# Attention beside expert tiles on one core: contiguous products for TensorE's sums, two more pairs in the first stretch, four tiles a step

## What is computed

```python
q = (x @ Wq + bq).reshape(B, T, H, Dh)                    # H = 16, Dh = 8
kv = ((x @ Wdown + bdown) @ Wup + bup).reshape(B, T, H, 2 * Dh)
k, v = jnp.split(kv, 2, axis=-1)
q, k = apply_rope(q), apply_rope(k)
att = jnp.einsum('bthd,btgd->bthg', q, k) / jnp.sqrt(Dh)
att = jax.nn.softmax(att, axis=-1)                        # over g, the heads
out = jnp.einsum('bthg,btgd->bthd', att, v)
return out.reshape(B, T, D) @ Wout + bout
```

```python
for e in range(E):
    h = gelu(x @ W_in[e] + b_in[e])
    out = out + combine[..., e, None] * (h @ W_out[e] + b_out[e])
```

## Time and profile before

| | us |
|---|---|
| median of three runs (1363.98 to 1368.10) | 1367.02 |
| the profiled execution | 1364.03 |
| its span in the trace | 1362.1 |
| TensorE busy, whole span | 1123.0 (82%) |
| VectorE busy | 831.2 (61%) |
| GpSimd busy | 796.9 (59%) |
| ScalarE busy | 596.3 (44%) |
| granted TensorE clock, mean | 0.954 of full |

### The profile page before, as it was taken

The page is one execution under the profiler, slowest core; times in us unless marked ns, Lnnn a source line. Parts: engine busy times, 40 slices in busy tenths (PEclk is TensorE's granted clock), DMA queues, the critical chain, the costliest instruction groups (busy, mean ns, idle before and its releaser), DMA issues.

```text
span 1362.1 us, 19492 instructions
## 1 busy us (share of the span) xinstructions
PE 1123.0 (82%) x6608; PEld 873.0 (64%) x6608; DVE 831.2 (61%) x1139; ACT 596.3 (44%) x1529; POOL 796.9 (59%) x613
## 2 busy tenths in 40 slices
PE   1448999999998988988783458899869999999975
PEld 1432222223887776777672457799868899899965
DVE  7946999997999999999998975111121000000038
ACT  0120011112766566656564448800005666656667
POOL 4605877873889899989881004767533445445520
PEclk9998999999999999999995779999989999999988
DMA  5471332131454554554445420199995767777747
GB/s 174 161 298 64 112 115 111 51 102 33 143 165 145 155 147 147 162 150 152 136 130 196 155 92 30 53 296 327 317 338 145 204 203 202 205 204 202 203 187 216
DMA packets 119955, 225.63 MB, mean 166 GB/s; under 512 B 16709, under 2 KB 80101, under 8 KB 117810
## 3 DMA queue, kind: packets, MB, share of 16 engines
q1 hardware_dynamic: 102164, 188.16, 44.9%
q0 software_dynamic: 17344, 35.57, 7.2%
q10 hardware_dynamic: 350, 0.67, 0.2%
HBM read 157.19 MB, written 67.14 MB: 165 GB/s over the span
## 4 chain that ended last, share of the span: by engine, by line
PE 42%; POOL 24%; DVE 11%; DMA 10%; ACT 6%; issue 6%; SPq 1%; POOLq 0%; ACTq 0%; DVEq 0%
PE ps L721 14%; POOL BG L259 12%; POOL y_tok L429 12%; PE ps L679 9%; PE ps L692 9%; DMA TPB<-in_kpad 5%; DVE XN L893 3%; DMA FF<-sorted_x 2%; PE ps L803 2%; DVE stats L863 2%; PE ps L805 2%; PE ps L668 1%; PE ps L730 1%; DMA xt_d<-xT 1%; DVE X L1037 1%
## 5 line engine op out<-in xcount | busy, mean ns | idle before, releaser
L429 POOL DMA_INDIRECT y_tok<-FF,yidx x284 | 306.9, 1081 | 206.0 <-ACT FF L497 146.0
L421 POOL DMA_INDIRECT sorted_x<-XN,idx x256 | 278.8, 1089 | 90.1 <-issue 89.0
L692 PE MATMUL ps<-FF 128*128 128x128 f32 x2272 | 278.8, 276 | 0.0
L692 PEld LDWEIGHTS ps<-FF 128*128 128x128 f32 x2272 | 266.9, 193 | 14.4 <-issue 4.3
L679 PE MATMUL ps<-FF 128*128 128x256 f32 x1136 | 273.8, 385 | 0.0
L488 ACT ACTIVATE FF<-ps,FF 128x256 f32<-128x256 f32 x568 | 230.2, 481 | 34.0 <-PE ps L679 33.1
L679 PEld LDWEIGHTS ps<-FF 128*128 128x128 f32 x1136 | 208.5, 194 | 23.3
L721 PE MATMUL ps<-BG,cst 128*128 128x512 f32 x208 | 193.3, 1097 | 0.0
L1146 DVE TENSOR_TENSOR BG<-BG,ps 128x512 f32<-128x512 f32 x16 | 10.6, 686 | 290.6 <-PE ps L837 290.4
L259 POOL TENSOR_TENSOR BG<-TPB 128x2048 f32<-128x2048 f32 x38 | 171.6, 4515 | 25.6 <-DVE BG L1028 13.6
L1016 DVE TENSOR_TENSOR BG<-BG,TPB 128x1024 f32<-128x1024 f32 x128 | 147.8, 1215 | 0.0
(11 more groups left out here) (185 smaller groups left out, 1676.7 us busy)
## 6 DMA issues: line engine op xcount, KB each, us to landing
FF<-in_moe SPq DMA_DIRECT2D x142, 514.0 KB
TPB<-in_kpad SPq DMA_DIRECT2D x22, 1024.0 KB, 7.8
sorted_x<-TPB SPq DMA_DIRECT2D x36, 516.0 KB, 4.1
FF<-sorted_x SPq DMA_DIRECT2D x142, 129.0 KB
FF<-in_kpad SPq DMA_DIRECT2D x10, 1024.0 KB
BG<-y_tok SPq DMA_DIRECT2D x8, 1024.0 KB, 6.6
X<-y_tok SPq DMA_DIRECT2D x8, 1024.0 KB, 6.5
y_tok<-FF,yidx POOLq DMA_INDIRECT x284, 3.2
```

The lines of the kernel that those rows point to most:

```text
L421: pool.indirect_dma_start(sorted_x[layer], bass.IndirectOffsetOnAxis(ap=idx[:, k, j:j + 1], axis=0), XN[:, j, :], None).then_inc(s_sc, 16)
L429: pool.indirect_dma_start(y_d[layer], bass.IndirectOffsetOnAxis(ap=yidx[:, G % 4, r:r + 1], axis=0), ys[:, G % 4, r * D:(r + 1) * D], None ...
L692: t = pe.matmul(psY[:, r * P:(r + 1) * P], hT[:, G % 2, m, r * P:(r + 1) * P], wc[:, G % 4, HID + m * D:HID + (m + 1) * D], start=False, s ...
```

## The change

TensorE's part grows. Products are laid out so that every pass of the score sum reads contiguous runs: ScalarE's evacuation of a projection tile now reorders `q` and `k` to feature-major (and `v` of the first 13 pairs to head-major) by two copies in place of one, and `own_product` writes its products feature by feature. The weighted products of pairs 0 to 12 (`PVS = 13`) are written in eight blocks of 512 and summed by TensorE too (`sum_values`, in the bank `psO`); VectorE reduces the remaining 512 to 256 in the next step (`finish_heads`). The scores have one bank, `psS`, in place of two, so a score sum waits until the one before has been read. `OWN` goes from 13 to 15 and `T_FIRST` from 12 to 14. From `T_FIRST` on a step has four tiles. Of the pairs from 15 on, GpSimd makes both half products of the even ones, and only the first of the odd ones; VectorE makes the second itself, in two instructions. GpSimd's first half product now waits for the weighted products of pair `b - 2`, not for its scaled heads.

```diff
-OWN = 13
-T_FIRST = 12
+OWN = 15
+PVS = OWN - 2
+T_FIRST = 14
+PER_STEP = 4
 def tiles_of(b):
-    f0, f1 = (7 * (b - T_FIRST + i) // 2 for i in range(2))
-    return [f for f in range(max(f0, 0), min(f1, NF))]
+    f0 = PER_STEP * (b - T_FIRST)
+    return [f for f in range(max(f0, 0), min(f0 + PER_STEP, NF))]
+def on_pool(b):
+    return 0 if b < OWN else 2 - b % 2
...
-        psS = [psH[2], psH[3]]
+        psO, psS = psH[2:4]
...
                 if b + 1 < NPAIR:
                     pool.wait_ge(s_qkv, 2 * (b + 1) + 2)
-                    pool.wait_ge(s_on, b - 1)
+                    pool.wait_ge(s_pv, b - 1)
                     qk_product(pool, b + 1, 0).then_inc(s_pp, 1)
                 for f in late[:2]:
                     scatter_outputs(0, f)
-                if b + 1 < NPAIR:
+                if b + 1 < NPAIR and on_pool(b + 1) == 2:
...
-                act.copy(qkv[:, m % 4, t, :], bank[:, 0:3 * D]).then_inc(s_qkv, 1)
+                if m < OWN:
+                    act.copy(qkv[:, m % 4, t, 0:2 * D].rearrange("p (a e h) -> p a e h", a=2, e=DH),
+                             bank[:, 0:2 * D].rearrange("p (a h e) -> p a e h", a=2, e=DH))
+                    v, vp = qkv[:, m % 4, t, 2 * D:3 * D], bank[:, 2 * D:3 * D]
+                    if m < PVS:
+                        v, vp = v.rearrange("p (g e) -> p g e", g=H), vp.rearrange("p (e g) -> p g e", e=DH)
+                    act.copy(v, vp).then_inc(s_qkv, 1)
+                else:
+                    act.copy(qkv[:, m % 4, t, :], bank[:, 0:3 * D]).then_inc(s_qkv, 1)
...
                 if G == 1:
                     pe.wait_ge(s_sub, OWN)
+                    pe.wait_ge(s_on, PVS)
...
             def sum_products(b):
                 pe.wait_ge(s_own, b + 1)
-                wait(pe, s_sub, b - 1)
-                pr = prod[:, b % 2, :].rearrange("p (n e) -> p e n", e=DH)
+                wait(pe, s_sub, b)
+                pr = prod[:, b % 2, :].rearrange("p (t e n) -> p e t n", t=2, e=DH)
...
+            def sum_values(b):
+                pe.wait_ge(s_pv, b + 1)
+                wait(pe, s_on, b)
+                pv = prodv.rearrange("p (i n) -> p i n", i=DH)
+                for i in range(DH):
+                    t = pe.matmul(psO[:, :], ident, pv[:, i, :], start=(i == 0), stop=(i == DH - 1))
+                t.then_inc(s_O, 1)
...
+                    if c == 0 and 2 <= b < PVS + 2:
+                        sum_values(b - 2)
                     if c == 0 and 3 <= b < NPAIR + 3:
                         heads_T(b - 3)
...
-                    dve.wait_ge(s_pp, 2 * (b - OWN) + 2)
+                    if on_pool(b) == 1:
+                        dve.wait_ge(s_qkv, 2 * b + 2)
+                        qk_product(dve, b, 1, 0, H // 2)
+                        link(qk_product(dve, b, 1, H // 2, H // 2))
+                    dve.wait_ge(s_pp, sum(on_pool(i) for i in range(b + 1)))
...
+            def finish_heads(b):
+                dve.wait_ge(s_O, b + 1)
+                link(dve.tensor_reduce(O, psO[:, :].rearrange("p (i n) -> p n i", i=2), AX.X, ALU.add))
+                scale_heads(b, O)
...
+                if 2 <= b < PVS + 2:
+                    finish_heads(b - 2)
                 if b >= 1:
-                    weighted(b - 1)
+                    (weighted_for_pe if b - 1 < PVS else weighted)(b - 1)
```

More of the change, by code:

```diff
@@ L212, in mixed_layers @@
         s_S = sem("scores_psum")
+        s_O = sem("heads_psum")
         s_sub = sem("scores_ready")
@@ L717, in sum_products @@
                 pe.wait_ge(s_own, b + 1)
-                wait(pe, s_sub, b - 1)
-                pr = prod[:, b % 2, :].rearrange("p (n e) -> p e n", e=DH)
+                wait(pe, s_sub, b)
+                pr = prod[:, b % 2, :].rearrange("p (t e n) -> p e t n", t=2, e=DH)
                 for e in range(DH):
-                    t = pe.matmul(psS[b % 2][:, :], ident, pr[:, e, :], start=(e == 0), stop=(e == DH - 1))
+                    t = pe.matmul(psS[:, :].rearrange("p (t n) -> p t n", t=2), ident, pr[:, e, :, :],
+                                  start=(e == 0), stop=(e == DH - 1))
                 t.then_inc(s_S, 1)
+            def sum_values(b):
[5 more added lines that the diff above has]
+                t.then_inc(s_O, 1)
             def qkv_tile(m, t, bank=psQ):
@@ L984, in own_product @@
                 dve.wait_ge(s_qkv, 2 * b + 2)
+                n = DH // 2
                 for t in range(2):
-                    for h0 in (0, H // 2):
-                        i = qk_product(dve, b, t, h0, H // 2)
+                    for e0 in (0, n):
+                        q = qkv[:, b % 4, t, e0 * H:(e0 + n) * H].rearrange("p (e h) -> p e h", e=n)
+                        k = qkv[:, b % 4, t, D + e0 * H:D + (e0 + n) * H].rearrange("p (e g) -> p e g", e=n)
+                        o = t * 2048 + e0 * H * H
+                        i = dve.tensor_tensor(
+                            prod[:, b % 2, o:o + n * H * H].rearrange("p (e h g) -> p e h g", e=n, h=H),
+                            q[:, :, :, None].to_broadcast([P, n, H, H]), k[:, :, None, :].to_broadcast([P, n, H, H]),
+                            ALU.mult)
                 i.then_inc(s_own, 1)
@@ L1007, in add_heads, with pair_sums, scale_heads, weighted_for_pe @@
                 dve.tensor_tensor(xv, xv, psA[:, 0:256], ALU.add).then_inc(s_xup, 1)
+            def pair_sums(b):
+                dve.wait_ge(s_exp, b + 1)
+                return mark(dve.tensor_reduce(Sm, S[:, b % 2, :].rearrange("p (n g) -> p n g", g=H), AX.X, ALU.add))
+            def scale_heads(b, heads):
+                wait(dve, s_ot, b - 2)
+                dve.tensor_tensor(On[:, b % 3, :].rearrange("p (n e) -> p n e", e=DH), heads.rearrange("p (n e) -> p n e", e=DH),
+                                  Rc[:, :, None].to_broadcast([P, 2 * H, DH]), ALU.mult).then_inc(s_on, 1)
+            def weighted_for_pe(b):
+                summed = pair_sums(b)
+                wait(dve, s_O, b)
+                for t in range(2):
+                    v = qkv[:, b % 4, t, 2 * D:3 * D].rearrange("p (g e) -> p g e", g=H)
+                    sc = S[:, b % 2, t * 256:(t + 1) * 256].rearrange("p (h g) -> p g h", h=H)
+                    pv = prodv.rearrange("p (g t h e) -> p t g h e", g=H, t=2, h=H)
+                    for g0 in (0, H // 2):
+                        n, g1 = H // 2, g0 + H // 2
+                        i = dve.tensor_tensor(pv[:, t, g0:g1, :, :],
+                                              sc[:, g0:g1, :, None].to_broadcast([P, n, H, DH]),
+                                              v[:, g0:g1, None, :].to_broadcast([P, n, H, DH]), ALU.mult)
+                i.then_inc(s_pv, 1)
+                dve.wait_ge(s_v, summed)
+                link(dve.reciprocal(Rc, Sm))
+            def finish_heads(b):
+                dve.wait_ge(s_O, b + 1)
+                link(dve.tensor_reduce(O, psO[:, :].rearrange("p (i n) -> p n i", i=2), AX.X, ALU.add))
+                scale_heads(b, O)
             def weighted(b):
-                dve.wait_ge(s_exp, b + 1)
-                summed = mark(dve.tensor_reduce(Sm, S[:, b % 2, :].rearrange("p (n g) -> p n g", g=H), AX.X, ALU.add))
+                summed = pair_sums(b)
                 for t in range(2):
```

8 lines of the change are left out of this document (3 added, 5 removed).

## The result

| | before | after |
|---|---|---|
| median, us | 1365.59 (8 runs, 1362.06 to 1369.27) | 1371.60 (8 runs, 1370.17 to 1375.26) |
| span of the profiled execution, us | 1362.1 | 1369.0 |
| first `hidden` at, us | 335.5 | 351.65 |
| last scatter of the layer at, us | 719.99 | 718.68 |
| combination begins at, us | 727.34 | 734.83 |

The ratio is 1.0048, 95% interval 1.0031 to 1.0065, so the changed kernel is slower by a little. The prediction had said 1352 us, faster than before; the measured time still lies inside its range of 1336 to 1373, but on the slower side of the kernel before. Behind the combination nothing changed: 1362.1 - 727.3 = 634.8 us before, 1369.0 - 734.8 = 634.2 now. So all of it happened ahead of that point.

A forecast was written before the change was run, and what follows sets the result against it. GpSimd was taken to bound the part with expert tiles: 35.0 us won there less 20.8 lost at its start gains 14.2, from 1364.03 to 1349.8 profiled; with the median 3.0 above, 1352 us was predicted, range 1336 to 1373.

The forecast's parts named there:

- What bounds the kernel: TensorE, 97% busy, from 106 to 338 us (stretch 1); GpSimd from 355 to 700 us (stretch 2), 19.43 us a step.
- The contiguous passes: Score sum on TensorE: reading contiguous runs, a pass takes 0.43 us instead of 0.918, a group of 16 takes 6.9.
- rival (d): Matmul passes stay at 0.918 us, a step before the expert tiles is 33 us, time about 1570; chance 0.02.
- VectorE in stretch 1: Attention steps before the tiles: VectorE's work falls to 13.1 us a step; its saving of 3.7 isn't on the path.
- ScalarE's copies: Evacuation of a projection tile: two copies take 1.0 us instead of one of 0.48, adding 0.5 a step for TensorE.
- The start of the tiles: The first `hidden` comes at 356.3 us instead of 335.5, behind the last value sum: 20.8 us later.
- The two steps laid out by hand: Steps with expert tiles: VectorE loses 3.65 us at its subtraction, GpSimd's later product costs nothing; 38.5 us for two.
- The rule of the Trainium skill: VectorE instructions with two SBUF inputs and GpSimd instructions reading SBUF take turns, whole instructions each; descriptor writing is inferred unaffected.
- Rival (a): VectorE's own halves collide with GpSimd's product in every second step: 21.3 us a step, 1383 us; chance 0.18.
- The forecast's step: A step with four expert tiles takes 19.5 us, bounds 18.7 and 20.1.
- What ends the layer: Last scatter at 705.8 us, then the load of its rows, then the combination; VectorE's own way ends earlier, at 711.
- The sign by which to tell: VectorE's two half products at 1.2 us each speak for the forecast, one of 4 to 5 for Rival (a).

## Why the prediction was wrong, point by point

- **What bounds the kernel** was right: GpSimd in stretch 2, TensorE in stretch 1. The run with all products on GpSimd at four tiles a step took 41.4 for two steps with 0.1 us idle.
- **The contiguous passes**, 0.43 each, 6.9 a group: 6.87 measured, for both sums. The rival (d) fell at once.
- **VectorE in stretch 1** was right in size (it waits 4.2 us a step). The prediction saw that the saving isn't on the path and that the price is, but didn't work out what the value sum costs: 14 to 16 us at the first `hidden`.
- **ScalarE's copies** were a mis-sized term: 1.0 taken, 0.64 measured (0.37 + 0.27), and 0.53 from start to end, hardly more than the 0.48 of the one copy. The nearer rows would have been that copy, from the same bank, and the kernel's other copies of 256 columns out of PSUM, of 0.37 to 0.40 us (L480, L497 and L508 before), not the later ones of 0.61 and 0.43. The step came out at 17.09 instead of 17.45, pair 14's sum ended at 343.55 instead of 348.3, and the first `hidden` stood at 351.65 instead of 356.3. This error was in the kernel's favour.
- **The start of the tiles**: 16.1 us later instead of 20.8.
- **The two steps laid out by hand** carry the failed step. Counted from the release of GpSimd's second product (462.36 - 42.86 = 419.50, one period before the row shown), VectorE's halves began at 25.06 (forecast 25.2) and GpSimd was ready at 25.84 (forecast 26.1 to 26.6, a little late). The times are right, and so is that GpSimd is ready while VectorE is in its halves. Wrong is the overlap that was concluded from them, "the product then runs under the reduction and costs nothing". It treats two instructions as one hold. The prediction had itself said that the share is held for a whole instruction, and the rows bear it out: the first half ended, the waiting GpSimd product got its turn, and the second half waited 4.3 us. For the two steps: 38.5 + 4.3 = 42.8, and 42.86 measured; with the collision taken away 38.65 and 38.47.
- **The rule of the Trainium skill** (SBUF — State Buffer, Who interferes with whom), that the shared read interface goes to whoever starts first, for a whole instruction, agrees with every collision here: 4.34 for the subtraction, 1.2 and 5.5 for the halves, 5.88 for GpSimd behind the one long instruction. Its inference that such a VectorE instruction leaves descriptor writing alone doesn't forecast the scatters: one under VectorE's weighted products takes 1.96 us, others 0.96. Whether it waits there to write descriptors or to read its row numbers `yidx`, the trace doesn't tell. GpSimd came 0.78 us after the start of the halves; 1.7 us sooner it would have been ahead of them, and by an estimate from the same rows VectorE would then have waited 3.6 us (4.5 less the 0.9 by which GpSimd was ahead), not much less than the 4.3.
- **Rival (a)** had named this, "gets the pair between the two halves", with its price: 42.6 for two steps and 1383 us. Measured were 42.86 and 1371.6. The collisions themselves cost what it had said, 28.8 us beside 30.6; the 11 us between 1383 and 1371.6 are nearly the 10 by which the kernel without collisions (1342.1) is below the forecast. Its chance of 0.18 was too small by the prediction's own numbers. The argument "for it: the margin is only about 1 us" was about GpSimd coming before the halves. Inside them what counts is the end of the first half, at 25.2 + 1.2 = 26.4: a product that is ready before it gets in between, one that comes after it waits. The forecast of 26.1 to 26.6 lies on both sides of that, so there was no margin at all. The first odd pair shows the other side: there GpSimd came 1.21 us behind the start, and VectorE's second half went first.
- **The forecast's step** of 19.5 us is what the kernel does without the collision: 38.47 / 2 = 19.24 with one instruction, the 38.5 of the hand layout. The 14.2 us of gain forecast became 23.7 in the median there. By the forecast the combination was to begin at 727.34 - 14.2 = 713.1; it began at 706.18, through a first tile 2.5 us sooner (353.81 in that run, 356.3 forecast) and the shorter step (17 x 0.26 = 4.4). The rest lies in the medians. A small slip of its own: 1349.8 + 3.0 is 1352.8, not 1352.
- **What ends the layer** was forecast wrong too. The last scatter was to stand at 705.8 with the combination behind the load of its rows, and "VectorE's own way" at 711, "under the load". In both kernels, with the collision and without, VectorE's way ended last: without it the last scatter stands at 690.17 and VectorE's last addition of heads at 705.72, directly ahead of the combination at 706.18. This didn't change the sign, but it is why the collisions came through to the time one by one.
- **The sign by which to tell** was well chosen: "two half products at 1.2 each would speak for the forecast, one of 4 to 5 us for (a)". One of 5.5 it was.

## What to carry to other kernels

When two engines take turns at a shared port, lay out single instructions, not groups: every boundary between two of one engine's instructions is a place where the other gets in with a whole one of its own. Give the engine that ends the stretch one long instruction, or hold the other back by a semaphore until its group is done; either was worth 27 to 29 us here. And before work is moved off an engine, look whether that engine or the one that takes it ends the stretch.

## What was not expected of the hardware

- GpSimd's product got its turn between two of VectorE's instructions that stand directly behind each other, in all seven cases in which it was clearly waiting then (6.66 to 6.68 us for the two halves, each time). The run without the value sum shows eight more.
- ScalarE's copies with a stride on the PSUM side were no dearer than those without: 0.37 us for 256 columns, as the contiguous copy of 256 (0.37, L505), and 0.27 for 128, beside 0.48 for 384 contiguous ones. VectorE's reduction of 512 elements from PSUM with a stride took 0.69, as the contiguous maximum.
- For TensorE the stride of its moving operand in SBUF decided: 0.43 us a pass of 512 float32 columns read as runs of 256, 0.918 with every eighth element, both at a granted clock of 0.98 to 0.99 in the stretch.
- Without the value sum, where TensorE waits for VectorE in every step of stretch 1, its granted clock there was 0.85 on average instead of 0.98, and a score sum behind a wait of 3.25 us took 10.09 us instead of 6.87. What was taken off TensorE didn't come back whole as idle time of TensorE.
